# A two-layer attention kernel whose second layer takes the key mask from TensorE to VectorE's maxima

## The reference

```python
xn = layer_norm(x, norm_w, norm_b)
q = (xn @ q_w + q_b).reshape(Bx, Tx, H, -1)
k = (xn @ k_w + k_b).reshape(Bx, Tx, H, -1)
att = jnp.einsum('bnhl,bmhl->bnmh', q, k)
mask = src_mask.reshape(Bx, 1, Tx, 1)
att = att + (1.0 - mask) * -1000000.0
att = jax.nn.softmax(att, axis=2)
v = ((xn @ v_w + v_b) * src_mask[:, :, None]).reshape(Bx, Tx, H, -1)
y = jnp.einsum('bnmh,bmhl->bnhl', att, v).reshape(Bx, Tx, Dx)
e = jax.nn.silu(emb) @ emb_w + emb_b
scale, shift = jnp.split(e[:, None, :], 2, axis=2)
h = layer_norm(y, sb_norm_w, sb_norm_b) * (1.0 + scale) + shift
h = jax.nn.silu(h) @ out_w + out_b
return x + h
```

## Time and profile before

| what | value |
|---|---|
| median of three runs | 2019.82 us (2018.45 to 2020.42) |
| the profiled execution, own time | 2020.07 us |
| its span | 2018.1 us |
| PE / PEld busy | 99% / 85% |
| DVE / ACT / POOL busy | 69% / 57% / 30% |
| second layer's mask products (L1801), 1200 to 1800 us | 148, mean 494 ns |
| reductions (L1402) | 256, mean 678 ns |
| exponentials (L1619) | 1024, mean 400 ns; accumulator reads 241 ns |
| the first layer's fused maxima (L838) | 256, mean 286 ns; accumulator reads 83 ns |

### The profile page before, as it was taken

The page is one execution under the profiler, slowest core; times in us unless marked ns, Lnnn a source line. Parts: engine busy times, 40 slices in busy tenths (PEclk is TensorE's granted clock), DMA queues, the critical chain, the costliest instruction groups (busy, mean ns, idle before and its releaser), DMA issues.

```text
span 2018.1 us, 52452 instructions
## 1 busy us (share of the span) xinstructions
PE 1991.9 (99%) x19377; PEld 1722.4 (85%) x19377; DVE 1384.3 (69%) x3505; ACT 1146.9 (57%) x3806; POOL 595.8 (30%) x985
## 2 busy tenths in 40 slices
PE   7999999999999999999999999999999999999998
PEld 5888888888888888888888888888888888888886
DVE  6777777777777777777666666666565666666665
ACT  4333433334333443344777777777777777777775
POOL 3333333333333332335122222222222222222220
PEclk9999999999999999999999999999999999999999
DMA  7310111101111011113111010101010101011000
GB/s 228 118 47 35 41 42 47 47 34 42 42 47 47 34 42 42 47 47 102 35 34 42 21 42 24 38 26 37 26 37 26 37 26 37 26 36 39 24 32 22
DMA packets 54856, 90.55 MB, mean 45 GB/s; under 512 B 4333, under 2 KB 17257, under 8 KB 54825
## 3 DMA queue, kind: packets, MB, share of 16 engines
q1 hardware_dynamic: 54800, 90.12, 13.3%
q10 hardware_dynamic: 24, 0.01, 0.0%
HBM read 56.46 MB, written 33.65 MB: 45 GB/s over the span
## 4 chain that ended last, share of the span: by engine, by line
PE 95%; DVE 2%; ACT 1%; SPq 1%; DMA 1%; issue 0%; POOL 0%; POOLq 0%; DVEq 0%
PE bank L545 16%; PE bank L547 14%; PE bank L546 14%; PE bank L554 9%; PE bank L555 9%; PE bank L556 9%; PE bank L566 7%; PE bank L1832 3%; PE bank L1807 3%; PE bank L1171 3%; PE bank L1157 2%; PE bank L1764 2%; PE bank L1801 1%; PE bank L1842 1%; PE bank L1066 1%; PE bank L503 0%
## 5 line engine op out<-in xcount | busy, mean ns | idle before, releaser
L554 PE MATMUL bank<-xT_hi,w_hi 128*128 128x256 f32 x1536 | 450.2, 293 | 1.1 <-DVE v L525 0.6
L555 PE MATMUL bank<-xT_lo,w_hi 128*128 128x256 f32 x1536 | 440.3, 287 | 0.0
L556 PE MATMUL bank<-xT_hi,w_lo 128*128 128x256 f32 x1536 | 437.5, 285 | 0.0
L1619 ACT ACTIVATE heads<-bank,top 128x128 f32<-128x128 f32 x1024 | 358.4, 400 | 88.2 <-DVE top L1402 88.0
L980 ACT ACTIVATE heads<-heads,k_neg 128x128 f32<-128x128 f32 x256 | 78.8, 389 | 453.2 <-POOL k_neg L720 453.2
L545 PE MATMUL bank<-w_hi,xT_hi 128*128 128x512 f32 x768 | 307.6, 401 | 4.6 <-DVE bias_all L391 4.6
L554 PEld LDWEIGHTS bank<-xT_hi,w_hi 128*128 128x128 f32 x1536 | 294.1, 192 | 10.8 <-issue 5.1
L547 PE MATMUL bank<-w_lo,xT_hi 128*128 128x512 f32 x768 | 301.3, 392 | 0.0
L546 PE MATMUL bank<-w_hi,xT_lo 128*128 128x512 f32 x768 | 300.9, 392 | 0.0
L555 PEld LDWEIGHTS bank<-xT_lo,w_hi 128*128 128x128 f32 x1536 | 294.6, 192 | 0.2 <-issue 0.2
L556 PEld LDWEIGHTS bank<-xT_hi,w_lo 128*128 128x128 f32 x1536 | 294.6, 192 | 0.0
(11 more groups left out here) (202 smaller groups left out, 3738.9 us busy)
## 6 DMA issues: line engine op xcount, KB each, us to landing
xr<-in_x SPq DMA_DIRECT2D x32, 512.0 KB, 3.5
x_between_layers<-ends SPq DMA_DIRECT2D x64, 256.0 KB, 2.0
xr<-x_between_layers SPq DMA_DIRECT2D x32, 512.0 KB, 4.1
out<-ends SPq DMA_DIRECT2D x64, 256.0 KB, 2.1
key_mask<-mask_parts SPq DMA_DIRECT2D x32, 128.0 KB, 3.3
store<-in_L_cond_W_emb SPq DMA_DIRECT2D x4, 1024.0 KB, 11.3
store<-in_L_cond_emb_w SPq DMA_DIRECT2D x3, 1024.0 KB, 7.7
mask_rows<-mask_parts SPq DMA_DIRECT2D x128, 2.0 KB
```

The source lines that it names most:

```text
L554: yield nc.tensor.matmul(dst, w_hi[:, m, c, fs], a_hi[:, c], start=(first and c == 0), stop=False)
L555: yield nc.tensor.matmul(dst, w_hi[:, m, c, fs], a_lo[:, c], start=False, stop=False)
L556: yield nc.tensor.matmul(dst, w_lo[:, m, c, fs], a_hi[:, c], start=False, stop=(last and c == C - 1))
L1619: last = nc.scalar.activation(prob[:, a, c, :], ps[a][:, c * P:(c + 1) * P], ACT.Exp, bias=top[:, b, h:h + 1], accum_out=total[:, b, h:h + 1])
```

## The change

In the second layer TensorE's four mask products in front of the scores fall away, and with them the mask's high and low parts, the row of ones and the four small mask loads of a pair. A pair's mask comes in one broadcast transfer into `key_mask1`, issued once the maxima of the pair before are all taken. VectorE's `maxima` now waits for all four banks at once, does a small copy, and then, for each of sixteen heads, one fused instruction: it adds the mask to the scores and flips the sign, writes the result to `prob` in SBUF, and takes the minimum into `top`; each increments `top`. ScalarE's `exps` read that SBUF result with a scale of -1, in place; in banks 0 and 3 they wait for `top` head by head, in banks 1 and 2 for four heads at once. In the last pair's second sequence the masked scores go to another tile.

Three orders change as well. In the even half, VectorE does `end_norm` ahead of `end_add`, and TensorE does the second sequence's values ahead of turning x, with its wait for `out` behind `prob_turned` rather than ahead of the z turnings. In the odd half, bank 3's maxima move behind `end_outputs`, the first two chunks of keys and `end_norm`.

```diff
@@ first_steps, vector
-        dve.wait_ge(mask_step, 4)
-        nc.vector.tensor_copy(mask_hi, mask_in).then_inc(mask_step, 1)
-        dve.wait_ge(mask_step, 5)
-        nc.vector.tensor_tensor(mask_lo, mask_in, f32(mask_hi), ALU.subtract).then_inc(mask_step, 1)
@@ layer1, sync
             if not last:
-                sp.wait_ge(s["s_ps"], seq(PAIR * C, i, PAIR * C))
-                sp.wait_ge(s["masks_in"], seq(16 * HC, i, 16 * HC))
-                load_masks(i + 1)
+                sp.wait_ge(s["top"], seq(PAIR * H, i, PAIR * H))
+                load_key_mask(sp, m.key_mask1, mask_d, 1, i + 1, s["masks_in"])
@@ layer1, vector
-        def maxima(i, b, some):
+        def maxima(i, b, some, masked=prob):
+            if some[0] == 0:
+                if b == 0:
+                    dve.wait_ge(s["masks_in"], seq(16, i, 16))
+                dve.wait_ge(s["s_ps"], seq(PAIR * C, i, b * C + HC))
+                nc.vector.tensor_copy(m.keys_seen[:, b:b + 1], eps[:, 0:1])
             for a in some:
-                dve.wait_ge(s["s_ps"], seq(PAIR * C, i, b * C + a + 1))
-                nc.vector.tensor_reduce(top[:, b, C * a:C * a + C],
-                                        ps[a][:, :].rearrange("p (c t) -> p c t", c=C), AX_X, ALU.max,
-                                        negate=True).then_inc(s["top"], 1)
+                for c in range(C):
+                    nc.vector.tensor_tensor_reduce(masked[:, a, c, :], ps[a][:, c * P:(c + 1) * P],
+                                                   m.key_mask1[:, b, :], -1.0, -LEAST, ALU.add, ALU.min,
+                                                   accum_out=top[:, b, C * a + c:C * a + c + 1])\
+                        .then_inc(s["top"], 1)
@@ step0
             maxima(i, 0, (3,))
+            end_norm(i - 1, 1)
             end_add(i - 1, slot_of(i - 1), 0)
-            end_norm(i - 1, 1)
             values(i, 0)
@@ step1
             end_outputs(i, 0)
-            maxima(i, 1, (3,))
             if first:
                 emb.leave_bank(dve, ps[EMB_BANK])
                 end_norm(i, 0)
             keys_out(i + 1, (0, 1))
             if first:
                 emb.gains(dve)
             else:
                 end_norm(i, 0)
+            maxima(i, 1, (3,))
             keys_out(i + 1, (2, 3))
@@ layer1, scalar
-        def exps(i, b, some=range(HC), turned=False):
+        def exps(i, b, some=range(HC), masked=prob):
             for a in some:
-                if turned:
+                if masked is not prob:
                     act.wait_ge(s["pT_ps"], seq(PAIR * C, i, a + 1))
-                act.wait_ge(s["top"], seq(PAIR * C, i, b * C + a + 1))
                 for c in range(C):
                     h = C * a + c
-                    last = nc.scalar.activation(prob[:, a, c, :], ps[a][:, c * P:(c + 1) * P], ACT.Exp,
+                    by_head = a in (0, HC - 1)
+                    if by_head or c == 0:
+                        act.wait_ge(s["top"], seq(PAIR * H, i, b * H + (h + 1 if by_head else h + C)))
+                    last = nc.scalar.activation(prob[:, a, c, :], masked[:, a, c, :], ACT.Exp, scale=-1.0,
                                                 bias=top[:, b, h:h + 1], accum_out=total[:, b, h:h + 1])
@@ layer1, tensor: scores
-            for a in range(HC):
-                rows = slice(DH * a, DH * a + 2)
-                nc.tensor.matmul(ps[a][:, :], one_rows[rows, :],
-                                 mask_rows[rows, b * P:(b + 1) * P].unsqueeze(1).broadcast_to([2, C, P]),
-                                 start=True, stop=False, tile_position=(DH * a, 0))
...
-                                            start=False, stop=(c == C - 1), tile_position=(DH * a, 0))
+                                            start=True, stop=True, tile_position=(DH * a, 0))
@@ layer1, tensor: step0
             pe.wait_ge(s["y"], seq(PAIR, i - 1, PAIR))
-            pe.wait_ge(s["out"], seq(PAIR, i - 1, 1))
             z_turned = z_transposed(i - 1, 1)
             run(islice(z_turned, C - 1))
             pe.wait_ge(s["prob"], seq(PAIR * C, i, C))
             run(z_turned)
             prob_turned()
-            x_turned()
+            pe.wait_ge(s["out"], seq(PAIR, i - 1, 1))
             pe.wait_ge(s["v"], seq(PAIR, i, 1))
             run(value_rows(i, 1))
+            x_turned()
```

More of the change, by code:

```diff
@@ L244, in sync @@
         sp.wait_ge(mask_out, 16)
-        load_key_mask(sp, m, mask_d, 0, s["masks_in"])
+        load_key_mask(sp, m.key_mask, mask_d, 0, 0, s["masks_in"])
         emb.load(sp, range(4))
[L247 to L250, removed]
         yield
@@ L462, in first_steps, with load_key_mask @@
     return dict(sync=sync, gpsimd=gpsimd, scalar=scalar, vector=vector, tensor=tensor)
-def load_key_mask(sp, m, mask_d, pair, arrived):
-    sp.dma_start(m.key_mask[:], mask_d[0, 0, bass.ds(pair * PAIR, PAIR)].unsqueeze(0).broadcast_to([P, PAIR, P]))\
+def load_key_mask(sp, tile, mask_d, layer, pair, arrived):
+    sp.dma_start(tile[:], mask_d[layer, bass.ds(pair * PAIR, PAIR)].unsqueeze(0).broadcast_to([P, PAIR, P]))\
         .then_inc(arrived, 16)
@@ L1198, in layer1 @@
     z, g, th, hs, h_hi, h_lo, y_out, v_bias, mask_now = m.z, m.g, m.th, m.hs, m.h_hi, m.h_lo, m.x1, m.v_bias, m.mask_now
-    one_rows, chunk_of, top, mask_rows = m.one_rows, m.chunk_of, m.top, m.mask_rows1
+    chunk_of, top = m.chunk_of, m.top
     def sb(name, shape):
@@ L1208, in layer1 @@
     prob_T = m.heads[:, H * P:2 * H * P].rearrange("p (a c t) -> p a c t", a=HC, c=C)
+    last_masked = m.pairs[:, 0:H * P].rearrange("p (a c t) -> p a c t", a=HC, c=C)
     total = sb("total", [P, PAIR, H])
@@ L1239, in sync @@
     def sync(sp):
-        def load_masks(pair):
-            for a in range(HC):
-                sp.dma_start(f32(mask_rows[DH * a:DH * a + 2, :]),
-                             mask_d[1, :, bass.ds(pair * PAIR, PAIR)].rearrange("r b t -> r (b t)"))\
-                    .then_inc(s["masks_in"], 16)
         def store(prev, b):
@@ L1562, in vector @@
         values(LAST, 0)
-        maxima(LAST, 1, (0, 1))
+        maxima(LAST, 1, (0, 1), last_masked)
         end_silu(LAST - 1, 1)
         prob_out(LAST, 0, 0, LAST_TURN_BANKS[0])
-        maxima(LAST, 1, (2, 3))
+        maxima(LAST, 1, (2, 3), last_masked)
         for a in (1, 2, 3):
@@ L1795, in scores @@
             if b == 0:
-                pe.wait_ge(s["masks_in"], seq(16 * HC, i, 16 * HC))
                 pe.wait_ge(s["q"], seq(2, i, 2))
                 pe.wait_ge(s["k"], seq(2, i, 2))
-            for a in range(HC):
-                rows = slice(DH * a, DH * a + 2)
-                nc.tensor.matmul(ps[a][:, :], one_rows[rows, :],
-                                 mask_rows[rows, b * P:(b + 1) * P].unsqueeze(1).broadcast_to([2, C, P]),
-                                 start=True, stop=False, tile_position=(DH * a, 0))
             for c in range(C):
```

27 lines of the change are left out of this document (11 added, 16 removed).

## The result

The changed kernel takes **2080.7 us** (median of four runs, 2079.11 to 2083.7) against 2020.12 us (2018.45 to 2020.86) for the kernel before on the same chip: ratio **1.0302, 95% interval 1.0289 to 1.0315**, so 3.0% slower. The sign of the forecast was right, the size was not: 2042 had been forecast, and 2080.7 lies above the range of 2016 to 2064.

A forecast was written before the change was run, and what follows sets the result against it. TensorE, busy 99% of the span, was taken as the bound, with exponentials nearly critical in both halves. Thirty loop pairs x +0.64 = +19.2, plus +2.9, made +22.1 us: forecast 2042 us, range 2016 to 2064.

The forecast's parts named there:

- Part 3: Layer 2's exponentials on ScalarE, reading SBUF: start every 0.30 us, bounded by 0.29 and 0.34; 0.34 before.
- Step 3: The claimed 0.30 us pace of ScalarE's exponentials from SBUF; starts 0.34 us apart or more would refute it.
- Part 1: TensorE in layer 2: dropping the mask products saves 0.34 us per half, 21.8 us in all if nothing else binds.
- Part 2: VectorE's maxima by head: fused instructions 0.21 us apart, reads 0.08 us; twelve heads finish 0.51 us later than before.
- Part 4: Odd half: bank 3's maxima behind keys and z's norm delay the last exponential and TensorE, +0.96 us, taken as +1.0.
- Part 5: Even half: TensorE's last wait, for prob or z, ends earlier, -0.36 us; moving x's turning costs nothing.
- Part 6: The rest: mask load nothing, opening taken as 0, first pair +3.3 and -0.6 us, last pair +0.2.
- the single terms: Terms outside the thirty loop pairs, for the first and last pair: +3.3 - 0.6 + 0.2 = +2.9 us.
- Slower exponentials: Rival: SBUF source makes ScalarE's step 0.38 us, odd half +1.2, even half gains nothing, about 2060 us; chance 0.08.
- The clock: Rival: a new 1.3 us gap per pair lowers TensorE's clock, +105 us, about 2145 us; chance 0.04.
- All kept: Rival: the late last bank costs nothing, so the mask products' whole saving stays, 1998 us; chance 0.17.
- half of it: Rival: head 13 comes some 0.7 us before the forecast time, the halves cancel, about 2020 us; chance 0.07.

The follow-up runs named there:

- the best order: Changed kernel with bank 3's maxima directly behind the outputs, the norm ahead of the keys (odd half), x turned directly behind prob (even half): 2037.16 us, ratio 1.0088.

## Why the prediction was wrong in size

The sum had +0.64 us per loop pair; it is +1.79. By its own parts:

- **Part 3 failed, and it is the largest error.** It took 0.30 us for a step and called 0.29 and 0.34 its bounds. They are no bounds: one row had the SBUF source without the sum, the other the sum without the SBUF source, and the table of four shows that the costs add to 0.387, outside both. The part even had the rule that says so, and set it aside because "the two rows here disagree with it"; they differed by the sum as well. In the odd half three steps follow the late bank: 3 x 0.087 = +0.26. In the even half fifteen follow the first: last minus first is 5.80 us, where it had 5.31 to 5.43. Without the sums, with the steps at 0.29, the kernel measured 2063.8, so their length is 16.9 of the 38.7 us by which the forecast of 2042 fell short. Its own sign had said so: "Step 3 is wrong if exponentials start 0.34 us apart or more".
- **Part 1 was too high:** 0.34 per half forecast, 0.23 measured by itself.
- **Part 2 was right on the instruction** (0.21 apart, reads of 83 ns, 1,024 of them) **and too early in its start.** VectorE starts 1.32 us after the scores begin (1255.50 - 1254.18), not 1.14 (1205.41 - 1204.27): the scores take longer to the last bank, which is part 1's 0.12 and some 0.06 more. That makes +0.18 in both halves.
- **Part 4 was right in its mechanism:** outputs, keys, a new wait for GpSimd's root (0.17 forecast as 0.23), norm, bank 3, an idle ScalarE (1.17 us; 2 was forecast, with quicker steps in front) and an idle TensorE (1.25, forecast 1.3). With the steps of parts 2 and 3 put right, +0.96 + 0.18 + 0.26 = 1.40 against the measured 1.42. The order is 0.92 of it, shown by undoing it alone.
- **Part 5 failed in sign:** -0.36 forecast, +0.37 measured. The wait for `prob` ends 8.04 us after the scores instead of 1228.03 - 1220.52 = 7.51: 0.18 for the start, the rest for fifteen slower steps. That is 0.15 later than the 7.89 of before. The other 0.16 to 0.25 is the turning of x, which the part took at nothing because it "moves the same TensorE work". The work is the same, its seams are not. The part also had z ready too soon: its turnings start 7.49 us behind the scores, not 1227.76 - 1220.52 = 7.24. So even at steps of 0.29 the even half gains nothing, with x's turning where the change puts it (16.84 us without the sums, 16.67 before).
- **Part 6, the first pair:** 2.7 forecast, 5.2 measured. The queries' products come 984.27 - 959.66 = 24.61 us after the pair's first scores, before 981.46 - 960.84 = 20.62, so +3.99. Of this the even half is +0.34, where it should save 0.6, and the way from the odd half's scores to the queries +3.65, where +3.3 was forecast. From there to the next pair's scores it takes 9.73 us instead of 8.54, so +1.19. The 1.6 us of the clock, which no part had, are in it, and a wait of 0.23 us that the kernel before has there is gone. The last pair has +1.5 where +0.2 was forecast. The mask load was nothing, as forecast: the changed kernel's waits have no line for it.

One sum of the prediction doesn't come out: 0.58 to 0.75 us per pair and 3 us on the single terms give 2037 to 2048, not 2034 to 2050. Nothing hangs on it.

**The rivals.** "Slower exponentials" named the cause of the largest error and gave 2060, because it let the even half break even and knew nothing of x's turning nor of the start. It got 0.08, for one row against it that did not speak to the question. "The clock" came true only behind the first pair's 3.71 us gap; 1.25 us in every pair did not lower it. "All kept" and "half of it" needed head 13 in time, and it came later than forecast (1261.80 - 1254.18 = 7.62 us against 1211.70 - 1204.27 = 7.43).

Left open: what makes the scores take 0.12 us longer to the next product without the mask products in front of them, whether it is the SBUF source or the writing over it that makes the step longer, and how the last 0.47 us per pair of the best order divides between slower steps and VectorE's longer queue.

## What to carry to other kernels

Before two rows are used as bounds, list every property in which they differ from the case; where they differ in two, the costs may add and the case lies outside both. An engine that reaches its wait with under 0.1 us of slack turns every delay of the chain beside it into time, so ask what three or fifteen steps of the uncertain length do, not one. When the order of a queue is changed, try each move alone: here one move of one call was over half of the loss, and the part meant to save time, by itself, did save 17 us.

## What the runs showed of the hardware that was not expected

- Exponentials of 128 columns start every 0.26 us from PSUM and every 0.29 from SBUF, and a row sum adds 0.09 to either (0.344, 0.387).
- VectorE's fused add and minimum of 128 columns starts every 0.21 us when it writes to SBUF, and every 0.25 when it writes back to its bank in PSUM; its accumulator read takes 83 and 140 ns.
- A change between turnings of 64 rows and full products costs TensorE some 0.1 us (0.32 instead of 0.23 in front of the turnings, 1.14 instead of 1.05 behind them).
- Four small products that run side by side ahead of a block took 0.34 us of its front and were worth 0.23 when gone.
